# Decoder layer in one kernel: x2 turned by DMA, the out bias on GpSimd, one VectorE branch, last product in halves, new orders and banks

## The reference

```
x = layernorm(x + attention(x))     # 16 query heads, 4 key heads of 16, RMS norm, rope, causal; out projection + bo
x = layernorm(x + wkv(x, context))  # per channel, over 128 steps: y_t = (e1*aa + e2*v_t) / (e1*bb + e2)
x = layernorm(x + ffn(x))           # h = relu(x @ sign(up).T * up_scale), 1024 wide
                                    # h @ sign(down).T * down_scale * output_scale
```

## Time and profile before

| | |
|---|---|
| median of 3 runs | 178.46 us |
| span of the profiled execution | 178.1 us |
| TensorE busy (matmuls) | 157.8 us, 89% |
| VectorE busy | 156.5 us, 88% |
| ScalarE busy | 138.9 us, 78% |
| GpSimd busy | 83.4 us, 47% |
| granted TensorE clock, mean | 0.979 of full |
| HBM | 9.52 MB read, 2.10 MB written, 65 GB/s over the span |

### The profile page before, as it was taken

One profiled execution on the slowest core, in us unless ns is written; L12 is line 12 of the kernel. 1 busy time (PEld: TensorE's weight loads), 2 busy tenths in 40 slices (PEclk: granted clock), 3 DMA queues, 4 the chain that ended last, 5 costly groups with the idle time before them and its releaser, 6 DMA issues.

```text
span 178.1 us, 3837 instructions
## 1 busy us (share of the span) xinstructions
PE 157.8 (89%) x1388; PEld 107.8 (61%) x1388; DVE 156.5 (88%) x289; ACT 138.9 (78%) x280; POOL 83.4 (47%) x109
## 2 busy tenths in 40 slices
PE   7978769989999999999999999999969798999920
PEld 2445424545645645566886668769758687898810
DVE  1489679798789999999899999999999999999981
ACT  3745488988998889999899989696687897898700
POOL 8282601017404695020873623699679457270121
PEclk9999969999999999999999999999999999999995
DMA  5899039044709107941070310000300010001122
GB/s 175 244 320 392 5 62 209 2 92 75 249 0 95 56 2 94 212 127 48 0 151 0 75 48 2 0 4 0 118 0 4 0 59 0 36 27 61 63 79 107
DMA packets 17989, 14.65 MB, mean 82 GB/s; under 512 B 12656, under 2 KB 13616, under 8 KB 17712
## 3 DMA queue, kind: packets, MB, share of 16 engines
q1 hardware_dynamic: 17424, 13.87, 29.8%
q10 hardware_dynamic: 544, 0.50, 0.9%
HBM read 9.52 MB, written 2.10 MB: 65 GB/s over the span
## 4 chain that ended last, share of the span: by engine, by line
PE 48%; DVE 27%; ACT 10%; issue 8%; DMA 3%; POOL 2%; SPq 0%; POOLq 0%; DVEq 0%; ACTq 0%
PE banks L417 9%; PE banks L576 8%; PE banks L500 7%; PE banks L597 6%; PE banks L533 5%; DVE hid_lo L1760 5%; DVE state L1702 4%; PE banks L472 4%; ACT probs L971 3%; DMA probs<-biases_dram 3%; DVE ratio L1712 2%; DVE stats L1676 2%; PE banks L510 2%; ACT dn_sb L918 2%; PE banks L479 2%
## 5 line engine op out<-in xcount | busy, mean ns | idle before, releaser
L971 ACT ACTIVATE probs<-banks 128x1024 f32<-128x1024 f32 x32 | 31.8, 1022 | 4.8 <-PE banks L479 4.8
L597 PE MATMUL banks<-dn_sb,hid_hi 128*128 128x256 bf16 x128 | 29.1, 272 | 1.1 <-DVE hid_lo L1760 1.1
L576 PE MATMUL banks<-x2hi,up_sb 128*128 128x256 f16 x128 | 29.1, 273 | 0.8 <-DVE x2lo L1753 0.5
L597 PE MATMUL banks<-dn_sb,hid_lo 128*128 128x256 bf16 x128 | 29.1, 273 | 0.0
L576 PE MATMUL banks<-x2lo,up_sb 128*128 128x256 f16 x128 | 29.0, 272 | 0.0
L417 PE MATMUL banks<-wqkv_sb,xT_sb 128*128 128x384 f32 x64 | 23.5, 512 | 2.0 <-issue 1.6
L1355 POOL TENSOR_SCALAR veps<-stats 128x2 f32<-128x2 f32 x24 | 9.4, 394 | 27.8 <-DVE stats L1676 26.8
L1361 POOL TENSOR_TENSOR rstd<-veps,half_neg 128x2 f32<-128x2 f32 x24 | 20.4, 853 | 1.3
L1019 ACT ACTIVATE banks<-banks,ups_man 128x256 f32<-128x256 f32 x48 | 19.6, 470 | 1.8 <-PE banks L576 1.6
L417 PEld LDWEIGHTS banks<-wqkv_sb,xT_sb 128*128 128x128 f32 x64 | 12.4, 201 | 11.9 <-issue 3.4
L1702 DVE TENSOR_TENSOR_SCAN state<-dec_sb,ke 128x1032 f32<-128x1032 f32 x8 | 18.4, 2301 | 0.0
(11 more groups left out here) (129 smaller groups left out, 355.8 us busy)
## 6 DMA issues: line engine op xcount, KB each, us to landing
ctxT_sb<-ctxT_dram SPq DMA_DIRECT2D x8, 256.0 KB, 3.1
x_sb<-x_dram SPq DMA_DIRECT2D x8, 256.0 KB, 3.8
out_dram<-outb SPq DMA_DIRECT2D x8, 256.0 KB, 2.2
xT_sb<-xT_dram SPq DMA_DIRECT2D x7, 256.0 KB, 4.4
up_f<-up_dram SPq DMA_DIRECT2D x1, 1024.0 KB, 6.4
dn_f<-down_dram SPq DMA_DIRECT2D x1, 1024.0 KB, 8.4
wqkv_sb<-wqkv_dram ACTq DMA_DIRECT2D x2, 192.0 KB, 3.1
xT_sb<-xT_dram SPq DMA_DIRECT2D x2, 128.0 KB, 2.9
```

What stands on the lines that cost most here:

```text
L576: mm = nc.tensor.matmul(banks[:, UP[p][n], s * T * S:(s + 1) * T * S], up_sb[:, c, j * 128:(j + 1) * 128], part[:, c, :, :].rearrange("p t ...
L597: mm = nc.tensor.matmul(banks[:, DN[p], t * D:(t + 1) * D], part[:, t * S:(t + 1) * S], down_of(j), start=(j == 0 and t == 0 and m == 0), ...
L971: nc.scalar.activation(probs[:, (T * p + t) % PROBS_N, 2 * h:2 * h + 2].rearrange("p n j s -> p n (j s)"), banks[:, b:b + 2], ACT.Exp).the ...
```

## The change

What it does, part by part:

- Pairs 0 to 5: x2 is split into high and low while tokens are on partitions (`x2h`, SBUF), by ScalarE or GpSimd (high) and GpSimd or VectorE (low), and one transposing DMA on SP (`x2_rows`) turns both parts into `x2T`, which ffn_up reads. Pairs 6 and 7 keep TensorE's transposes.
- The out bias is no longer a product: GpSimd adds it to x_sb in eight `add_bias`; `residual` waits for that. The bias of q, k, v is loaded to three partitions only, after VectorE has cleared the tile; SP issues the gains' load.
- VectorE has one branch around two whole orders, as TensorE has; TensorE's value load and branch move behind `first_rows`.
- `hidden` lies in one of two SBUF buffers for 31 of 32 quarters (`HID`). Of the splits, 12 high_bits move from ScalarE to GpSimd and 16 low_bits from VectorE to GpSimd.
- The last pair's down product has one bank for each sequence; its last quarter is done sequence after sequence (`ffn_down_half`), with `scale_half`, `add_half` and `store_half` behind it.
- The orders of all engines and the banks are new. In the new ones ScalarE's list begins masks, squares(0), decay_rates, take_values(0), up_signs, mean_log(0), first_root(0), squares(1), down_signs, take_values(1), down_weights(0), down_weights(1), mean_log(1), first_rows_out, first_root(1), take_values(2), take_values(3), now_gains, squares(2), exps(0, 0, 0); VectorE's branch begins with small_constants.

```diff
+        X2_BY_DMA = (1, 1, 1, 1, 1, 1, 0, 0)
...
+        HID = ((1, 0, 1, 0), (0, 1, 0, 0), (1, 0, 1, 0), (1, 0, 1, 0), (1, 0, 1, 0), (1, 0, 1, 0), (1, 0, -1, 1), (1, 0, 1, 0))
...
+            if HID[p][n] >= 0:
+                return hid[:, HID[p][n]]
...
+            def x2_rows(p):
+
+                done(sp, "x2lo_done", p)
+                sp.dma_start_transpose(x2T[:, p % X2T_N].rearrange("p a t c s -> p (a t c) s"),
+                                       x2h[:, p % X2H_N].rearrange("p a t c d -> p (a t c d)")).then_inc(arrival("x2_in", p), 16)
...
+            def store_half(p, t):
+
+                done(sp, "out_done", p, t + 1)
+                sp.dma_start(out[p][:, t], outb[:, p % OUT_N, t]).then_inc(last_stored, 16)
...
+            sp.wait_ge(bias_clear, 1)
+            for r in (0, 32, 64):
+                sp.dma_start(bias_in[r:r + 1], biases.partition_broadcast(1)).then_inc(bias_in_done, 16)
+            for dst, src in gain_loads:
+                sp.dma_start(dst, src).then_inc(gains_in, 16)
...
+            x2_rows(0)
...
-                nc.tensor.matmul(banks[:, WO[p]], ones_b[:], bias_rows[:, E:E + D].unsqueeze(1).to_broadcast([BR, T, D]),
-                                 start=True, stop=False)
...
+                if X2_BY_DMA[p]:
+                    landed(pe, "x2_in", p)
+                else:
+                    done(pe, "x2lo_done", p)
+                if p == 0 and n == 0:
+                    pe.wait_ge(up_ready, 1)
...
+            def ffn_down_half(p, t):
+
+                n = NJ // 2 - 1
+                hidden_there(p, n)
+                for s in range(2):
+                    j = 2 * n + s
+                    for m, part in enumerate((hid_hi, hid_lo)):
+                        mm = nc.tensor.matmul(down_tile(p, t), part[:, j, t * S:(t + 1) * S], dn_sb[:, j],
+                                              start=False, stop=(s == 1 and m == 1))
+                mm.then_inc(sems["dn_mm"], 1)
...
             masks()
             squares(0)
+            decay_rates()
             take_values(0)
-            take_values(1)
+            up_signs()
             mean_log(0)
             first_root(0)
             squares(1)
-            high_heads(0)
+            down_signs()
+            take_values(1)
+            down_weights(0)
+            down_weights(1)
             mean_log(1)
+            first_rows_out()
             first_root(1)
+            take_values(2)
+            take_values(3)
+            now_gains()
             squares(2)
-            take_values(2)
-            swap_keys(0)
...
+            def add_bias(p):
+
+                landed(pool, "x_in", p)
+                if p == 0:
+                    pool.wait_ge(params_in, PARAMS)
+                rows_of = x_sb[:, p % X_N]
+                nc.gpsimd.tensor_tensor(rows_of, rows_of, bo_b[:].unsqueeze(1).to_broadcast([128, T, D]), ALU.add)\
+                    .then_inc(sems["xb_done"], 1)
...
+            def high_x2(p):
+
+                done(pool, "x2_done", p)
+                nc.gpsimd.tensor_copy(x2h[:, p % X2H_N, 0].rearrange("p t c d -> p (t c d)"),
+                                      x2[:, p % X2_N].rearrange("p t d -> p (t d)")).then_inc(signal("x2hi_done", p), 1)
+
+            def low_x2(p):
+
+                done(pool, "x2hi_done", p)
+                high, low = [x2h[:, p % X2H_N, part].rearrange("p t c d -> p (t c d)") for part in range(2)]
+                nc.gpsimd.tensor_tensor(low, x2[:, p % X2_N].rearrange("p t d -> p (t d)"), high, ALU.subtract)\
+                    .then_inc(signal("x2lo_done", p), 1)
+
+            def high_bits(p, n):
+
+                done(pool, "hid_done", p, 2 * n + 2)
+                nc.gpsimd.tensor_copy(hid_hi[:, 2 * n:2 * n + 2], hidden(p, n)).then_inc(signal(f"hi{n}_done", p), 1)
...
+            def scale_half(p, t):
+
+                done(dve, "dn_mm", p, NJ // 2 + t)
+                nc.vector.tensor_tensor(down_tile(p, t), down_tile(p, t), dsc_b[:], ALU.mult).then_inc(sems["o3_done"], 1)
+
+            def add_half(p, t):
+
+                done(dve, "o3_done", p, t + 1)
+                nc.vector.tensor_tensor(r3[:, p % R3_N, t], down_tile(p, t), x2[:, p % X2_N, t], ALU.add)\
+                    .then_inc(signal("r3_done", p), 1)
...
+            plain = dve.value_load(flags[0:1, 0:1], min_val=0, max_val=1)
+
+            def from_heads(guarded):
+
+                small_constants()
+                head_sums(0)
+                rope_sines(0)
+                rope_cosines(0)
+                rope_sum(0)
+                newton_rms(0)
+                scale_heads(0)
+                rope_sines(1)
+                low_heads(0)
+                swap_keys(0)
+                head_sums(1)
...
+                low_bits(7, 0)
+                done(dve, "out_done", 4)
+                scale_out(6)
+                add_out(6)
+                moments(2, 6)
+                low_bits(7, 2)
+                low_bits(7, 3)
+                landed(dve, "stored", 4)
+                normed(2, 6)
+                scale_half(7, 0)
+                add_half(7, 0)
+                scale_half(7, 1)
+                add_half(7, 1)
+                moments(2, 7)
+                landed(dve, "stored", 5)
+                normed(2, 7)
+
+            with dve.If(plain):
+                from_heads(False)
+            with dve.Else():
+                from_heads(True)
 
```

More of the change, by code:

```diff
@@ L1066, in _ @@
-            act.wait_ge(bias_out_ready, 4)
+            take_products(0, 1)
+            take_values(4)
             exps(1, 0, 0)
-            done(act, "pv_mm", 0)
-            take_values(4)
-            mean_log(3)
+            high_heads(3)
             exps(1, 0, 1)
-            take_products(0, 1)
-            first_root(3)
-            up_signs()
-            swap_keys(2)
+            mean_log(4)
+            first_root(4)
+            squares(5)
             exps(1, 1, 0)
-            now_gains()
+            exps(1, 1, 1)
@@ L1243, in _ @@
-            relu(5, 2)
-            done(act, "up_mm", 5)
-            high_x2(6)
+            high_bits(5, 2)
+            done(act, "lo1_done", 5)
             relu(5, 3)
@@ L1449, in _ @@
+            high_x2(0)
+            low_x2(0)
+            keys_by_context(2)
+            low_heads(6)
+            inverse_root(0, 3)
+            root(0, 3)
+            num_by_rec(1)
+            scale_heads(7)
+            add_bias(6)
+            high_heads(7)
+            low_bits(0, 0)
             low_heads(7)
-            inverse_root(0, 3)
-            den_by_rec(2)
+            low_bits(0, 1)
             inverse_root(1, 1)
             root(1, 1)
+            den_by_rec(2)
+            low_bits(0, 2)
@@ L1454, in _ @@
+            high_bits(0, 3)
+            high_x2(1)
+            low_x2(1)
             inverse_root(0, 4)
-            root(0, 3)
+            add_bias(7)
             root(0, 4)
-            add_out(0)
+            low_bits(0, 3)
             inverse_root(1, 2)
             root(1, 2)
-            keys_by_context(4)
+            den_by_rec(3)
             inverse_root(0, 5)
             root(0, 5)
-            low_bits(1, 2)
-            num_by_rec(3)
-            add_out(1)
-            den_by_rec(4)
@@ L1467, in _ @@
-            inverse_root(1, 3)
-            num_by_rec(4)
-            root(1, 3)
-            inverse_root(2, 0)
+            add_out(0)
+            high_bits(1, 0)
+            keys_by_context(4)
+            inverse_root(2, 0)
+            inverse_root(1, 3)
+            root(1, 3)
+            root(2, 0)
+            high_bits(1, 1)
+            low_bits(1, 2)
+            keys_by_context(5)
+            high_bits(1, 3)
+            high_x2(3)
+            den_by_rec(4)
+            low_x2(3)
@@ L1827, in _ @@
-            done(dve, "rscale_done", 4)
-            head_sums(5)
-            rope_sines(5)
-            attend_norm(1)
-            rope_cosines(5)
-            normed(0, 0)
-            rope_sum(5)
-            newton_rms(5)
-            keys_by_context(0)
-            scan(0)
-            residual(1)
-            mix(0)
-            with dve.If(guarded):
-                row_maxima(3)
-            moments(0, 1)
-            rope_sines(6)
-            rope_cosines(6)
-            attend_norm(2)
```

1299 lines of the change are left out of this document (628 added, 671 removed).

## The result

The changed kernel takes 211.06 us (210.19 to 211.46) against 178.3 for the kernel before on the same chip: 1.181 times as long, 95% interval 1.176 to 1.186. The forecast of 175.0 and its range up to 180.8 are both missed, and on the wrong side. The profiled execution has a span of 209.7 us. In all comparisons here, executions over 1.5% above the fastest of the same kernel count in the medians and not in the ratios.

What follows compares the result with a forecast made beforehand. TensorE and VectorE, both within 7% of full, were taken as bounds. Start 26.2 + TensorE's work 134.7 + gaps 6.8 + tail 6.6 = 174.3, plus 0.36 and 0.3 for small things: 175.0 us, range 170.5 to 180.8.

Steps and rivals of the forecast that it cites:

- gaps: TensorE's idle time between first score product and last matmul: 8.3 us before, forecast 6.8.
- so +2.3: Gaps added because VectorE's loss to GpSimd, 1.7 us before, was scaled by both busy times to 4; bounds 0 and 9.
- The turns: Streaming GpSimd instructions and VectorE instructions with two SBUF inputs take turns; those with a PSUM input don't. Charged 2.3 us.
- low_bits over 0.9 on average: Sign that the forecast is wrong: VectorE's low_bits averaging over 0.9 us, against 0.68 normally.
- VectorE's relief: VectorE loses 16 of 27 low_bits and three low_x2, falling from 139.4 to about 130 us; 3.3 us of gaps go.
- GpSimd not a bound: GpSimd rises from 83 to about 123 us busy, itself no bound over 170 us.
- The start: Up to the first score product: 26.2 us instead of 21.8, from later parameter loads and ScalarE's early signs and weights.
- TensorE's work: From first score product to last matmul: 140.3 to 134.7 us, without bias products (2.6) and six x2 transposes (3.0).
- this counts in full: TensorE's 5.6 us of saved work shorten the time fully, as TensorE is a bound, if VectorE keeps up.
- The transposing transfers: x2's path to ffn_up by DMA: 3.6 to 4.3 us per transfer, covered by another pair's quarters, charged 0.
- The tail: From last matmul to end: 7.65 to 6.6 us, by normed(2,6) moved earlier (0.73) and halves (about 0.3).
- take turns too often: Slow-side rival: in the FFN's last 65 us VectorE waits 9.6 us on GpSimd's streaming; 180 to 182 us, chance 0.23.

Runs made afterwards that it cites:

- kernel without streaming: Changed kernel, nearly all of GpSimd's streaming instructions replaced by products of a few columns, those computations left out: 177.96 us, 0.988 to 0.997 of the kernel before.
- small kernel: Separate kernel, eight VectorE instructions beside six of GpSimd, all 128x512: eight two-SBUF-input products take 4.91 us alone, 11.29 beside products.
- pow to short stand-ins: Changed kernel, 36 streaming GpSimd instructions replaced by equally long pow on few columns (197.44 us), then by short two-column products (191.99 us).

## Why the prediction was wrong

The reading by terms was not the fault. The changed kernel without streaming, cut at its first score and its last matmul, reads:

```profile
26.10:168.70 142.60, 135.48 (x1294) 96.55 (x1295) 131.66 (x233) 114.03 (x221) 79.17 (x123) 0.98 0.27 63
```

Start 26.1, work 135.5, gaps 7.1, tail 7.7: near the forecast's 26.2, 134.7, 6.8 and 6.6. It described a kernel in which GpSimd's new work costs VectorE next to nothing. Part of that nearness is luck. This kernel streams less on GpSimd than the kernel before, so by the forecast's own terms its gaps should be 6.8 without the 2.3, 4.5 at most. They are 7.1, so the other terms of the gaps were too hopeful by 2.6 us or more. The step that failed is "so +2.3": the price of the turns, 2.3 us of new gaps, where the gaps came to 30.4 instead of 6.8 and 33 us of the time leave with GpSimd's streaming.

*The turns.* Right: that two SBUF inputs take turns, that a bank frees an instruction from them, that the new SBUF buffers of hidden make takers of VectorE's ten low_bits. The prediction's own sign, low_bits over 0.9 on average, was nearly met (0.877). Wrong: the size. It took the 1.7 us that VectorE loses before as a price of chance meetings and scaled it by the two busy times. But the kernel before is placed so that streaming falls mostly beside instructions with a bank; the encounters of the earlier trace rows are the few exceptions. Eight additions in idle slots of GpSimd cost four times that sum, 6.9 us. A price by encounter was to be had from the same rows: 59.57 shows VectorE losing 1.05 us to one product of 1.26, and the small kernel gives 1.06. The prediction's own list puts 27 more products (16 low_bits, eight additions, three of x2) and 16 more casts on GpSimd; half of them meeting a taker would have been 13.5 x 1.06 + 8 x 0.41 = 18 us (an estimate), and the whole forecast another one. Left out as well: the tensor_scalar of normed, with one SBUF input, and the two-element offset pay too.

*VectorE's relief*, 3.3 us of gaps: this fell with the turns. A low_bits of 0.68 us moved to GpSimd gave VectorE back 0.68 and took 1.08 in the run with six of them.

*GpSimd not a bound*: it is busy 144 us, not 123, since its own instructions stretch too (low_bits 1372 ns against 1168 in the earlier trace rows), and it is at 18 to 19 of 20 us from 80 to 140. The step from pow to short stand-ins, 5.5 us at equal streaming, shows its queue as a cost of its own. Of two long waits in the changed kernel the first is for a VectorE that is late, the second for GpSimd's queue (engine and line, what for, total, times, longest):

```profile
PE banks L594 <- DVE ny L1805: 8.8, 5, 3.3
...
ACT hid L1062 <- POOL hid_lo L1436: 6.5, 7, 1.5
```

*The start.* The chain on ScalarE came as worked out: up_f landed at 16.1, mean_log(0) ran at 17.94 for a forecast of 17.9. Still the first scores came at 29.19, not 26.2, and ScalarE wasn't what held them. The step left out is a queue that an edit was moved into: add_bias(0) stands ahead of high_heads(0) on GpSimd and waits for x. In the changed kernel:

```profile
21.30 1.27 POOL L1368 TENSOR_TENSOR x_sb<-x_sb,bo_b 128x512 f32<-128x512 f32 x1 [6.49 <-DMA x_sb<-x_dram]
22.52 0.72 POOL L1387 CAST stack<-qn 128x640 f16<-128x640 f32 x1
23.19 3.07 POOL L1368 TENSOR_TENSOR x_sb<-x_sb,bo_b 128x512 f32<-128x512 f32 x2
23.27 1.88 DVE L1707 TENSOR_TENSOR stack<-qn,stack 128x640 f16<-128x640 f32 x1 [1.17 <-POOL stack L1387]
25.18 1.24 DVE L1716 COPY stack<-stack 128x128 f16<-128x128 f16 x2
```

The cast of the heads comes 2.2 us after VectorE's product was done at 20.3, and then low_heads takes 1.88 for 0.82 and the swap 1.24 for 0.29 beside the next additions. With the additions' streaming out, the first scores are at 25.1 to 26.1. That the forecast's 26.2 is met there is partly luck: with ScalarE's signs moved away too they come at 25.5, held by x's landing through GpSimd's queue, so two chains end within 0.6 us of each other, and the forecast had one. That the signs' early place pays something back in the full stretch was right: moved late in the kernel without streaming, with nothing else changed, they cost 3.5 us.

*TensorE's work.* The counts held, busy 154.4 us without streaming for a forecast of 152. The 142.4 us in the changed kernel come with a clock of 0.96 over the full stretch and 0.89 in the start, against 0.99 and 1.00 in the earlier trace rows. TensorE stood idle from 14.1 to 17.95 us and from 22.7 to 26.5, and the slices of the granted clock read 0.8 from 15.7 to 26.2 and 0.5, the lower level of 1.2 GHz, from 26.2 to 36.7. How much of the 6.9 us above 135.5 is the clock wasn't separated. But "this counts in full" was wrong for one part at least: taken alone, the bias product is worth nothing, most likely since VectorE, at 19 of 20 us between 60 and 160, sets the pace.

*The transposing transfers* were right at nothing: six landings of 2.7 us in the median, less than the 3.6 to 4.3 taken, and no wait for them among the longest. The Trainium skill's 1309 ns for one block ("VectorE: DVE Perf Modes", The three transpose paths), taken eight times, would be 10.5 us by estimate; the measurement decides for 2.7:

```profile
x2T<-x2h SPq DMA_TRANSPOSE x6, 2.7
```

*The tail*, 6.6, was 7.7. VectorE is late there, at normed(2, 6) until 202.1, so the half that is ready early helps nobody, and four halves take 1.7 us where scale and addition whole took 1.4. From the last matmul to the last normed it is 3.66 us for 4.02, so the order saved 0.36 of the 1.0 that was forecast; from there to the end, with two stores, it is 4.04 for 3.63, which gives that back.

*The rivals.* The one on the slow side, "take turns too often", had the mechanism, the right engine and its condition (about 5 us of waits), but at 180 to 182 it was 30 us off as well. It fell short for two reasons: it counted the FFN's last 65 us alone, and for each meeting half of GpSimd's 1.17 us where whole ones are paid. And the chance of 0.23 rested on the same scaling.

The Trainium skill, "GPSIMD Engine Reference", section Specifications, names contention for VectorE instructions with two SBUF inputs or in a two-port mode. The first half is seen: two inputs, 0.61 us to 1.41. One input is hit in one form, a normed of 0.42 us without streaming and 0.70 with it, and not in another, the statistics at 693 and 699 ns; that would fit the second half, but no run here shows in which mode either ran.

## What to carry to other kernels

An instruction with SBUF inputs alone moved from a full VectorE to an idle GpSimd need not save VectorE anything: here a low_bits cost it 1.08 us for 0.68, and a new addition 0.86. So look at what VectorE will run beside it, prefer places where that reads banks, and price the move by the encounter, not by shares of busy time. Before crediting TensorE's savings in full, look which engine is at 19 of 20. Look at the start too: three narrow bias rows and a later branch gave 1.9%, the only clear gain of a kernel here that computes everything. When work is moved onto a queue, look for what its first instruction waits and who stands behind it; and when a branch seems to cost time, look at the waits in front of it.

## What the runs showed of the hardware

- A pow over a few columns runs beside VectorE without a trace (4.91 us for eight products, as alone) though it keeps GpSimd for 1.18 us each; a two-element VectorE instruction is held for 0.9 us by one streaming GpSimd instruction. What counts for VectorE is the stream, not how long GpSimd is busy. The other way a short instruction is held as well: a two-column product of GpSimd, 0.20 us in the median, takes 2.09 from 129.67 in the kernel without streaming, until VectorE's scan (129.46, 2.30 us) has ended.
- Who pays is not symmetric. Beside sparse VectorE takers GpSimd's addition keeps its 1.28 us and VectorE pays; between dense ones GpSimd's stretches too: of its twelve products from 7.62 to 25.26 us in the small kernel, the six alone (up to 15.12) take 7.5 us, the six beside VectorE's 10.1.
- Where the later start was undone in the changed kernel, only 2.2 of 5.8 us came through. That it was GpSimd's load that took it back is argued, not shown: the run meant to tell it moved too little of the start.
